# Row-half transposes in the products' ring, cleared scratch behind the gathers, and a new order of steps in a DLRM tower

## The reference, cut to what matters

```
e = stack([tbl_f[ids[:, f]] for f in 32 fields], axis=1)     # 512 x 32 x 64
p, q = e[:, ids_x, :], e[:, ids_y, :]                        # all 496 pairs x < y
z = einsum('bpi,pij->bpj', p, w)                             # w: 496 x 64 x 64
z = einsum('bpj,bpj->bp', z, q)                              # 512 x 496
h = concatenate([z, dense_ctx], axis=1)                      # 512 x 512
h = maximum(h @ W_top1 + b_top1, 0)                          # 512 x 512
h = maximum(h @ W_top2 + b_top2, 0)                          # 512 x 256
y = h @ W_top3                                               # 512 x 1
```

## Time and profile before

| | before |
|---|---|
| median of three runs | 279.42 us |
| profiled execution, time / span | 276.6 / 274.8 us |
| PE, PEld busy | 212.6, 146.9 us |
| DVE, ACT, POOL busy | 175.4, 152.3, 150.2 us |
| mean granted TensorE clock | 0.944 of 2.4 GHz |

### The profile page before, as it was taken

One profiled execution on the slowest core, in us unless ns is written; L12 is line 12 of the kernel. 1 busy time (PEld: TensorE's weight loads), 2 busy tenths in 40 slices (PEclk: granted clock), 3 DMA queues, 4 the chain that ended last, 5 costly groups with the idle time before them and its releaser, 6 DMA issues.

```text
span 274.8 us, 7208 instructions
## 1 busy us (share of the span) xinstructions
PE 212.6 (77%) x2584; PEld 146.9 (53%) x2584; DVE 175.4 (64%) x160; ACT 152.3 (55%) x1146; POOL 150.2 (55%) x186
## 2 busy tenths in 40 slices
PE   0163300799789788799799879789987999999995
PEld 0052100455546376466458647467646787666884
DVE  0011000669676857688698776687887798989741
ACT  1010000336686768366963891916687697899601
POOL 4777774446564625455466554465661684677600
PEclk9998555599999999999999999999999999999999
DMA  6756754501110100101011110011110000000000
GB/s 242 257 192 203 276 214 168 174 11 27 19 27 16 26 14 19 22 17 24 18 17 23 22 26 12 14 26 20 26 22 13 18 4 4 2 1 1 2 2 3
DMA packets 6437, 15.29 MB, mean 56 GB/s; under 512 B 2689, under 2 KB 2945, under 8 KB 5250
## 3 DMA queue, kind: packets, MB, share of 16 engines
q1 hardware_dynamic: 2306, 10.62, 10.7%
q0 software_dynamic: 4096, 4.20, 7.6%
HBM read 14.82 MB, written 0.00 MB: 54 GB/s over the span
## 4 chain that ended last, share of the span: by engine, by line
PE 71%; issue 14%; DVE 5%; another core or an unknown queue 4%; POOL 3%; DMA 2%; ACT 1%; DVEq 0%
PE pu L489 22%; PE pu L497 22%; PE pz L514 14%; PE pt L521 5%; PE pt L464 3%; POOL emb L291 3%; PE pt L533 3%; DVE prod L416 2%; DVE turned L398 2%; DMA emb<-in_tbl,idx 1%; PE pu L521 1%; PE pt L543 1%; DMA idx<-in_ids 1%; PE pt L475 1%
## 5 line engine op out<-in xcount | busy, mean ns | idle before, releaser
L291 POOL DMA_INDIRECT emb<-in_tbl,idx x128 | 120.9, 944 | 97.6 <-PE pu L489 40.3
L319 ACT ACTIVATE turned<-turned 128x64 f32<-128x64 f32 x544 | 130.3, 245 | 3.2 <-issue 1.7
L319 ACT ACTIVATION_READ_ACCUMULATOR turned<-turned 128x1 f32 x544 | 103.9, 191 | 1.6 <-issue 1.4
L416 DVE TENSOR_TENSOR prod<-pu,eT 128x1024 f32<-128x1024 f32 x48 | 57.3, 1218 | 60.5 <-PE pu L497 35.4
L398 DVE TENSOR_TENSOR turned<-pu,emb 128x1024 f32<-128x1024 f32 x64 | 76.1, 1217 | 19.3 <-PE pu L489 19.0
L489 PE MATMUL pu<-ws,eT 64*128 64x512 f32 x256 | 69.9, 639 | 22.4 <-issue 18.7
L497 PEld LDWEIGHTS pu<-eT,ws 64*128 64x128 f32 x1024 | 64.3, 193 | 15.4 <-issue 12.9
L497 PE MATMUL pu<-eT,ws 64*128 64x128 f32 x1024 | 69.8, 283 | 2.8 <-issue 1.1
L310 ACT COPY eT<-pt 128x128 f32<-128x128 f32 (+1 forms) x28 | 11.2, 401 | 82.8 <-remote 34.4
L514 PE MATMUL pz<-prod,select 128*32 128x128 f32 x1024 | 41.4, 282 | 12.1 <-issue 12.0
L514 PEld LDWEIGHTS pz<-prod,select 128*32 128x32 f32 x1024 | 30.3, 112 | 25.4 <-issue 22.1
(11 more groups left out here) (24 smaller groups left out, 25.6 us busy)
## 6 DMA issues: line engine op xcount, KB each, us to landing
ws<-in_w SPq DMA_DIRECT2D x8, 1024.0 KB, 4.8
emb<-in_tbl,idx POOLq DMA_INDIRECT x128, 2.5
w1s<-in_w SPq DMA_DIRECT2D x1, 1024.0 KB
zT<-in_dense SPq DMA_DIRECT2D x1, 512.0 KB
w2s<-in_w SPq DMA_DIRECT2D x1, 512.0 KB
idx<-in_ids SPq DMA_DIRECT2D x1, 64.0 KB, 1.9
identity<-in_ident SPq DMA_DIRECT2D x1, 64.0 KB, 2.4
w3s<-in_w SPq DMA_DIRECT2D x1, 1.0 KB
```

Source lines behind the costliest of these rows:

```text
L291: nc.gpsimd.indirect_dma_start(out=emb[:, c % EC, x, :], out_offset=None, in_=tables[x], in_offset=bass.IndirectOffsetOnAxis(ap=idx[:, c, ...
L319: i = nc.scalar.activation(t, t, ACT.Copy, accum_out=zB[:, b // NT % 2, b % NT * 16 + v:b % NT * 16 + v + 1])
L416: nc.vector.tensor_tensor(p.rearrange("p x s b -> p x (s b)"), u.rearrange("p x s b -> p x (s b)"), e, ALU.mult).then_inc(mult_done, 1)
```

## The change

It has three parts, and a new set of hand-written orders for them.

The transposes of the pairs, and those of z of chunks 0 to 2, go through the ring `pu` in place of the bank `pt`. Each is done in two halves: batch rows 0 to 63 against the upper left quarter of the identity into the slot's first bank, rows 64 to 127 against the lower right quarter into its second bank. The ring now serves 171 fills (`FILLS`: 128 products, 40 groups of pairs, 3 of z) and not 128; a fill waits for whoever read the slot three fills ago. ACT's copy of a group reads both banks and raises `xt_read` or `zt_read`.

Later chunks turn two pairs at a time (`XN = [1, 2, 2, 2]`), so 24 groups in place of 12.

On POOL the wait for `u_ready` ahead of each gather of chunks 1 to 3 is gone. Behind each gather from the 17th on, POOL clears a scratch tile of 128 partitions by 256 columns and waits until that is done.

The tables `TURNED`, `TURN_AT`, `ROWS`, `X_AT`, `MLP_AT`, `SUMS_AT` and `Z_LATE` are all new. The number of row sums by engine changes from 34, 21 and 9 (ACT, DVE, POOL) to 38, 21 and 5.

```diff
-TURNED = [3, 4, 5, 8, 9, 10, 11, 12, 18, 19, 21, 22, 24, 27, 28, 29]
+TURNED = [2, 3, 4, 5, 8, 9, 10, 12, 13, 14, 18, 19, 22, 26, 27, 28]
...
-XN = [1, 4, 4, 4]
+XN = [1, 2, 2, 2]
...
-X_AT = [[-1, -1, -1, -1, -1, 1, 2, 4, 6, 8, 9, 12, 13, 14, 16, 23],
-        [27, 33, 39, 46],
-        [58, 60, 70, 74],
-        [83, 91, 99, 105]]
-
-MLP_AT = [(7, 11, 20, 23, 30), (14, 16, 22, 29, 31), (14, 18, 22, 25, 27)]
+X_AT = [[-1, -1, -1, -1, 0, 1, 1, 3, 6, 8, 9, 12, 13, 17, 18, 23], [25, 30, 32, 34, 38, 42, 46, 50], [58, 62, 63, 66, 71, 73, 78, 83], [87, 90, 96, 98, 103, 107, 113, 115]]
+
+MLP_AT = [(4, 9, 16, 30, 34), (6, 8, 14, 19, 35), (6, 14, 17, 23, 27)]
...
+FILLS = []
+for _t in range(-1, NS):
+    FILLS += [("u", _t)] if _t >= 0 else []
+    FILLS += [v for v in TURNS[_t] if v[0] == "x" or v[0] == "z" and v[1] < BCH - 1]
+FILL = {v: i for i, v in enumerate(FILLS)}
...
+        def turned_over(fill, n):
+
+            return pu[:, FILL[fill] % UR, :, 0:(n + 1) // 2, :].rearrange("p h s b -> p h (s b)")[:, :, 0:n * BH] \
+                .rearrange("p h (i b) -> p i h b", b=BH)
+
+        def slot_free(engine, fill):
+
+            if FILL[fill] >= UR:
+                what, v = FILLS[FILL[fill] - UR]
+                if what == "u":
+                    engine.wait_ge(mult_done, v + 1)
+                elif what == "x":
+                    engine.wait_ge(xt_read, v + 1)
+                else:
+                    engine.wait_ge(zt_read, v + 1)
...
                 for x in range(FIELDS):
-                    if c:
-
-                        pool.wait_ge(u_ready, (c - 1) * NU + x + 1)
                     if c >= EC and x == 0:
 
                         pool.wait_ge(mult_done, (c - EC + 1) * NU)
...
+                    if c * FIELDS + x >= PAUSE_FROM:
+
+                        n += 1
+                        nc.gpsimd.memset(pause[:], 0.0).then_inc(paused, 1)
+                        pool.wait_ge(paused, n)
...
-                nc.scalar.copy(eT[:, c % EC, k:k + n, :], pt[:, 0:n, :]).then_inc(pt_read, 1)
+                nc.scalar.copy(eT[:, c % EC, k:k + n, :].rearrange("p i (h b) -> p i h b", h=2),
+                               turned_over(("x", g), n)).then_inc(xt_read, 1)
...
-                u = pu[:, t % UR, :, :, :]
+                u = pu[:, FILL["u", t] % UR, :, :, :]
...
             def transpose_x(g):
                 c, k, n = GROUPS[g]
-                pt_free("x", g)
+                slot_free(pe, ("x", g))
+                to = turned_over(("x", g), n)
                 for i in range(n):
                     pe.wait_ge(s_emb[c * KP + k + i], 16 * 2)
-                    mm = nc.tensor.transpose(pt[:, i, :], emb[:, c % EC, 2 * (k + i):2 * (k + i) + 2, :].rearrange("p f e -> p (f e)"),
-                                             identity[:])
+                    for h in range(2):
+                        rows = slice(BH * h, BH * (h + 1))
+                        mm = nc.tensor.transpose(to[:, i, h, :], emb[rows, c % EC, 2 * (k + i):2 * (k + i) + 2, :]
+                                                 .rearrange("p f e -> p (f e)"), identity[rows, rows])
                 mm.then_inc(xt_ready, 1)
...
-                pe.wait_ge(pt_read, PLACE["x", GROUP_OF[c, UNITS[u][1]]] + 1)
-                if t >= UR:
-
-                    pe.wait_ge(mult_done, t - UR + 1)
+                pe.wait_ge(xt_read, GROUP_OF[c, UNITS[u][1]] + 1)
+                slot_free(pe, ("u", t))
```

More of the change, by code:

```diff
@@ L20 @@
 DENSE = 16
+BH = P // 2
 H1, H2 = 512, 256
@@ L115 @@
 EC = 2
+PAUSE = 256
+PAUSE_FROM = 16
 WU = 4
 W_AT_ONCE = 2
[L122 removed]
+XN = [1, 2, 2, 2]
 GROUPS = [(c, k, XN[c]) for c in range(BCH) for k in range(0, KP, XN[c])]
 NG = len(GROUPS)
[L129 to L136 removed]
+X_AT = [[-1, -1, -1, -1, 0, 1, 1, 3, 6, 8, 9, 12, 13, 17, 18, 23], [25, 30, 32, 34, 38, 42, 46, 50], [58, 62, 63, 66, 71, 73, 78, 83], [87, 90, 96, 98, 103, 107, 113, 115]]
+MLP_AT = [(4, 9, 16, 30, 34), (6, 8, 14, 19, 35), (6, 14, 17, 23, 27)]
+X_STEPS = [at for of_chunk in X_AT for at in of_chunk]
+USERS = [((c + 1) * NU + at, what, c) for c in range(BCH - 1) for what, at in zip(("l1a", "l1b", "l2", "l3"), MLP_AT[c][1:])]
 USERS += [((BCH - 1) * NU + Z_LAST, "z", BCH - 1)] + [(NS, what, BCH - 1) for what in ("l1a", "l2", "l3")]
[L138 to L139 removed]
+USERS.sort(key=lambda v: (v[0], v[2]))
 PLACE = {v[1:]: i for i, v in enumerate(USERS)}
+TURNS = {t: [] for t in range(-1, NS)}
+for _g, _t in enumerate(X_STEPS):
+    TURNS[_t].append(("x", _g))
+for _c in range(BCH - 1):
+    TURNS[(_c + 1) * NU + MLP_AT[_c][0]].append(("z", _c))
+for _t, _what, _c in USERS:
+    if _t < NS:
+        TURNS[_t].append((_what, _c))
+FILLS = []
[3 more added lines that the diff above has]
+FILL = {v: i for i, v in enumerate(FILLS)}
+NF = len(FILLS)
 GROUP_OF = {(c, k + i): g for g, (c, k, n) in enumerate(GROUPS) for i in range(n)}
[L143 removed]
+SUMS_AT = ((1, 4, 7, 11, 13, 17, 20), (1, 9, 11, 13, 14, 19, 22, 23, 24, 25, 26, 28), (0, 6, 7, 9, 16, 18, 19, 23, 26, 29, 31), (1, 6, 7, 11, 14, 19, 27, 31))
 SUMS_LATE = 2
@@ L190, in dlrm_tower @@
         y = sb("y", [1, BATCH])
+        pause = sb("pause", [P, PAUSE])
         pu = ps("pu", [P, UR, 2, 4, P])
@@ L206, in dlrm_tower @@
         pt_read = sem("pt_read")
+        xt_read = sem("xt_read")
+        zt_read = sem("zt_read")
         rows_act = sem("rows_by_scalar")
@@ L324, in copy_z @@
                 act.wait_ge(zt_ready, c + 1)
-                nc.scalar.copy(zT[:, ZA:ZCH, cols(c)], pt[:, 0:ZCH - ZA, :]).then_inc(pt_read, 1)
+                if c < last:
+                    nc.scalar.copy(zT[:, ZA:ZCH, cols(c)].rearrange("p i (h b) -> p i h b", h=2),
+                                   turned_over(("z", c), ZCH - ZA)).then_inc(zt_read, 1)
+                else:
+                    nc.scalar.copy(zT[:, ZA:ZCH, cols(c)], pt[:, 0:ZCH - ZA, :]).then_inc(pt_read, 1)
             def layer1(c, half):
@@ L402, in multiply @@
                 p = prod[:, a % PR, :, :, :]
-                dve.wait_ge(pt_read, PLACE["x", GROUP_OF[c, k]] + 1)
+                dve.wait_ge(xt_read, GROUP_OF[c, k] + 1)
                 if a >= PR:
@@ L474, in transpose_z @@
                 for i in range(ZCH - ZA):
-                    mm = nc.tensor.transpose(pt[:, i, :], zB[:, c % 2, i * P:(i + 1) * P], identity[:])
+                    if c == last:
+                        mm = nc.tensor.transpose(pt[:, i, :], zB[:, c % 2, i * P:(i + 1) * P], identity[:])
+                        continue
+                    to = turned_over(("z", c), ZCH - ZA)
+                    for h in range(2):
+                        rows = slice(BH * h, BH * (h + 1))
+                        mm = nc.tensor.transpose(to[:, i, h, :], zB[rows, c % 2, i * P:(i + 1) * P], identity[rows, rows])
                 mm.then_inc(zt_ready, 1)
@@ L488, in products @@
                         rows = slice(EMB * bank, EMB * (bank + 1))
-                        i = nc.tensor.matmul(pu[:, t % UR, bank, :, :], eT[rows, c % EC, UNITS[u][1], :], ws[rows, u, :, :],
+                        i = nc.tensor.matmul(pu[:, FILL["u", t] % UR, bank, :, :], eT[rows, c % EC, UNITS[u][1], :], ws[rows, u, :, :],
                                              start=True, stop=True)
@@ L496, in products @@
                         rows = slice(EMB * bank, EMB * (bank + 1))
-                        i = nc.tensor.matmul(pu[:, t % UR, bank, slot, :], ws[rows, u, slot, :], eT[rows, c % EC, k, :],
+                        i = nc.tensor.matmul(pu[:, FILL["u", t] % UR, bank, slot, :], ws[rows, u, slot, :], eT[rows, c % EC, k, :],
                                              start=True, stop=True)
```

21 lines of the change are left out of this document (12 added, 9 removed).

## The result

| | before | after |
|---|---|---|
| median of four runs | 278.66 us | 296.94 us |
| lowest and highest | 277.54, 279.53 | 293.93, 301.73 |
| profiled execution, time / span | 276.6 / 274.8 | 301.73 / 299.9 |

The changed kernel takes 1.063 times as long, with an interval of 1.058 to 1.069. The forecast was 246 us, with a range of 224 to 272. The profiled execution of the changed kernel is its slowest, 1.6% above the median of its runs and left out of the ratio, so I use it for where time goes, and the other runs for how much.

A forecast was written before the change was run, and what follows sets the result against it. Gathers 1.25 us apart hold back PE's signals, wholly in the first 50 us. Last landing 213.1, transposes 0.3, end 29.6: span 243.0, with 1.8 around it 244.8 us; median forecast 246, range 224 to 272.

The forecast's parts named there:

- one good row: After the gather at 60.14, 1.84 us behind another, a transpose ending at 61.46 is copied by ACT at 61.49.
- The row at 159.68: DVE's multiply of a product ended at 157.42, read as 2.3 us late, with gathers 1.24 us apart.
- C: Rival: the hold stays, gathers go on to the 64th; four steps at 104 us, span about 329 us; chance 0.07.
- B: Rival: signals late by a us or so but passing, 1.73 to 1.95 us a step; 255 to 270 us; chance 0.19.
- the start: Steps 0 to 23 on PE, step by step behind the gathers: done at 51 us, 1.33 us each.
- The fill and the cadence: POOL's clearing of 256 columns behind a gather: 0.35 us, making gathers 1.69 us apart.
- The gather-bound end: Span set by POOL's gathers, 55.5 + 111 x cadence; it passes 274.8 us at a cadence of 1.98 us.
- The end: From step 115 on, work as before: 29.6 us; POOL's row sums there fall from 9 to 5.
- Ring and copies: Copies queued behind ACT's row sums hold ring slots: 0 to 27 us for 27 fills, put at nothing on the path.

The follow-up runs named there:

- e2: The changed kernel without its cleared tile, and still without the waits for `u_ready`: 378.46 us, ratio 1.364 to the kernel before.
- the orders alone: The changed kernel with the waits for `u_ready` back and no cleared tile: 276.80 us, ratio 0.995 in a held session; 227.88 us, 1.042 in a free one.

## Why the prediction was wrong

**The reading of what bounds the kernel stands, in the main.** Gathers in close succession hold back PE: in the changed kernel nothing is held where gathers rest, no tile makes DVE's held time 103 us, a tile of 1024 columns makes it 4.8. That was shown by size and place, not only argued. But the prediction spoke of PE's signals alone, and PE's own matmuls are held as well (stops of 50.5, 7.0 and 0.2 us in the same three kernels).

**The step that failed** is the one sentence "The removed waits for `u_ready` cost nothing and no longer tie POOL to PE", together with the "one good row" beneath it, that "1.84 us between two of them leaves a signal free" and 1.69 would do as well. The waits for `u_ready` were what kept the hold short. They stopped the gathers at 45 us, and PE recovered. Without them the row of gathers runs on to the 64th, and signals in it come up to 7 us late: steps 0 to 23 were done at 98 us, not 51. A single pair at 1.84 us is no test for a long row. I had written that down as the weakness of the reading, and still gave the forecast 0.55.

The trace of before even had a row against it, between the same two gathers. A product ends at 59.01 us and an idle DVE multiplies it only at 59.90:
```profile
59.90 1.22 DVE L412 TENSOR_TENSOR prod<-pu,eT 128x1024 f32<-128x1024 f32 x1 [0.73 <-PE pu L489]
```
The row at 159.68 was read too strongly, too: the multiply was 2.3 us behind its product, but DVE was idle for only 0.90 of them.

**The rivals.** What happened is C's mechanism (the hold stays, and the gathers go on to the 64th) at B's strength (signals late but passing). C was priced at 329 us with the hold whole, B at 255 to 270 with a start only some us late. Neither reached 297: B had the late signals but a start "some us late", where it was 47; C had the start, and asked for a hold that never passes. e2, without the tile, is C in full, at 378 us: C's price left out that the later rows of gathers hold PE too (41 us of held time in the third alone). B and C together had 0.26. The right rival would have lain between them, with C's late start and B's step: 98.4 us, then 92 steps of 1.87 us (172.5 in all), then 29.6. That makes 300.5 us, but it only adds up what was measured.

**The fill and the cadence.** 0.326 us against 0.35, and 1.55 against 1.69. I had put the fill 0.10 us behind the gather, from the add at 219.05; it follows at once. The shorter cadence is on the side that holds. From 256 to 1024 columns a fill grows from 326 to 966 ns, 0.83 ns a column. The Trainium skill, GPSIMD Engine Reference, section Elementwise, side-by-side cycle accounting, has 1.03 cycles an element for simple bodies; an estimate from it, with its 1.2 GHz, is 0.86 ns a column, and the trace's 0.83 agrees.

**The gather-bound end.** 55.5 + 111 x cadence was right where it applied: 298.6 for 301.4 with the wide tile and, as a weaker test, 227.6 for 229.2 in the free session. In the run of the result the gathers weren't the bound; the last is issued at 233.5 us and step 115 is multiplied at 270.9.

**The end.** 29.0 us for 29.6, with five sums on POOL in place of nine. The clock stayed near full in the eighth slice, as said. What that gained doesn't show, since PE mostly waited there.

**Ring and copies "at nothing on the path".** In the held sessions that is so (0.995), since the held signals cover it. It is not so where the cover is gone. In the free sessions steps 24 to 115 take 140.7 us for the orders alone and 131.6 before, 9 us more, inside the 0 to 27 that I had for it. The transposes themselves came out on the cheap side: a group of two pairs in halves takes 0.22 us of PE's time, one of two whole transposes 0.37 (in the kernel with the new tables and `pt`), and one of four 0.59. These are medians from the group's first start to the next instruction's, in free sessions.

**In the free sessions** the start is near what I forecast: 19 multiplies by 50 us and step 24 at 57.5, where I had 24 by 51. But it is so in the kernel before as well (19, and 57.6), which leaves the change nothing to win. A version that beats the kernel before in both kinds of session wasn't found; the orders alone are 0.5% better in the held ones and 4.2% worse in the free ones.

## What to carry to other kernels

A wait that looks like mere coupling may be what gives another engine its rests: before counting its removal at nothing, ask what will run without a pause once it is gone, and how far. A spacing read off one pair of instructions is not a spacing that holds for a hundred. And measure the kernel before again beside every experiment: a change to an order that is tuned around a stall can look free while the stall covers it, and cost 4% once it is gone.

## What the runs showed of the hardware

*Indirect gathers on POOL and TensorE.* In the held kind of session, with gathers 1.25, 1.55 and 2.19 us apart behind the 17th, the three kernels with the same orders and no waits, profiled once each and not side by side, start 4, 5 and 16 multiplies in 49.5 us. DVE is held for 103, 53.5 and 4.8 us in all, and PE stops inside products and sums for 50.5, 7.0 and 0.2 us. In the changed kernel nothing is held where gathers rest. At 1.25 us the hold outlasts the row: a product of the first row is multiplied only at 91.73 us, 10 us behind the start of that row's last gather. Which part of a gather does it isn't known: plain DMAs from SP or POOL were only tried where nothing was held.

*The hold comes and goes for the same code.* The kernel before took 278 us in two sessions and 219 us in three, always within 1.2% of its median in one session; profiled, DVE is held for 44.0 us in the one kind and 0 in the other. That is 60 us, over three times what the whole change costs. What decides it stays open: it isn't the kernel, since all of them follow, and it isn't the chip's number alone, since one of the held sessions and one of the free ones have the same.

*Fills on POOL.* A fill of 128 partitions by 256 or 1024 float32 columns starts with no gap behind a gather, where a tensor operation had one of 0.10 us.
